# State-space layer with a mixture of experts: B and C rows spread over the partitions by one DMA each, and a different queue and place for three loads of the scan stage

## The reference, cut to what matters

```python
xi, res = split(x @ W_in);  xi = silu(causal_conv4(xi) + conv_b)
Bm, Cm = split(xi @ W_xproj)              # 16 + 16 numbers per token
delta = softplus(xi @ W_dt + b_dt);  A = -exp(A_log)
def step(h, inp):                         # one token after another
    u_i, d_i, B_i, C_i = inp
    dA = exp(d_i[:, None, :] * A[None, :, None])
    h = h * dA + d_i[:, None, :] * B_i[:, :, None] * u_i[:, None, :]
    return h, sum(h * C_i[:, :, None], axis=1)
y = (scan(step) + xi * D_param) * silu(res);  return y @ W_out
```

## Time and profile before

| | us |
|---|---|
| median of 2 runs | 8991.39 (8988.93 to 8993.84) |
| the profiled execution, its own time | 9033.67 |
| its span, on the slowest core (core 6) | 9032.1 |
| spans of the 8 cores | 8923.9 to 9032.1 |
| stage B on core 6, from the trace | 1938 to 6695 of the span |
| DVE busy, whole span | 4786.0 (53%) |
| PE busy, whole span | 3628.9 (40%) |
| the chain that ended last: DVE 46%, DMA 31%, PE 17% | |

### The profile page before, as it was taken

One profiled execution on the slowest core, in us unless ns is written; L12 is line 12 of the kernel. 1 busy time (PEld: TensorE's weight loads), 2 busy tenths in 40 slices (PEclk: granted clock), 3 DMA queues, 4 the chain that ended last, 5 costly groups with the idle time before them and its releaser, 6 DMA issues.

```text
span 9032.1 us, 43824 instructions; the slowest of 8 cores (8923.9 to 9032.1 us)
## 1 busy us (share of the span) xinstructions
PE 3628.9 (40%) x16374; PEld 1964.3 (22%) x16480; DVE 4786.0 (53%) x1407; ACT 1377.8 (15%) x1158; POOL 147.5 (2%) x213
## 2 busy tenths in 40 slices
PE   3886554520000000015345335435343348475665
PEld 2675444420000000002112112112110113132222
DVE  1211000018898888879889879779762222222222
ACT  0111111112222222222212112112110000000000
POOL 0000000000000000000000000000000000000000
PEclk9887777765555555557667667667676669797888
DMA  6334322231000111110120120120211148475664
GB/s 90 112 103 130 111 114 114 110 119 28 23 14 18 28 28 28 28 37 11 50 61 10 51 60 10 51 60 10 51 42 41 50 88 141 91 133 101 116 118 92
DMA packets 175006, 603.59 MB, mean 67 GB/s; under 512 B 38974, under 2 KB 56510, under 8 KB 146670
## 3 DMA queue, kind: packets, MB, share of 16 engines
q0 software_dynamic: 126752, 293.81, 16.8%
q1 hardware_dynamic: 48046, 306.98, 10.7%
HBM read 546.28 MB, written 168.43 MB: 79 GB/s over the span
## 4 chain that ended last, share of the span: by engine, by line
DVE 46%; DMA 31%; PE 17%; issue 3%; ACT 2%; another core or an unknown queue 1%; DVEq 0%; SPq 0%; POOLq 0%; ACTq 0%
DVE h_b L102 24%; DVE dBu L102 12%; DMA wr<-WrT 9%; DVE y_acc L102 6%; PE PP L490 5%; DMA Bb_b<-Bb_b 4%; DMA Cb_b<-Cb_b 3%; PE PP L896 2%; PE PP L382 2%; DMA u_b<-u_sp 2%; PE PP L437 1%; PE PP L397 1%; DMA wr<-WsT 1%; PE PP L717 1%; DMA du_sp<-du_b 1%
## 5 line engine op out<-in xcount | busy, mean ns | idle before, releaser
L626 PE MATMUL PP<-y_acc,sid 128*128 128x512 f32 x2048 | 1196.2, 750 | 3560.9 <-DVE y_acc L102 3560.9
L102 DVE TENSOR_TENSOR_SCAN h_b<-dAb,dBu 128x4112 f32<-128x4112 f32 x256 | 2233.4, 8724 | 197.5 <-ACT dBu L102 167.9
L626 PEld LDWEIGHTS PP<-y_acc,sid 128*128 128x128 f32 x2048 | 489.0, 246 | 4267.5 <-issue 4267.5
L102 DVE TENSOR_TENSOR dBu<-du_b,Bb_b 128x4096 f32<-128x4096 f32 x256 | 1132.8, 4425 | 419.7 <-DMA Bb_b<-Bb_b 392.9
L102 ACT ACTIVATE dAb<-d_b,A_bc 128x4096 f32<-128x4096 f32 x256 | 950.5, 3713 | 617.7 <-DMA d_b<-d_sp 594.5
L896 PE MATMUL PP<-ue,wr 128*128 128x512 bf16 x4012 | 913.0, 386 | 218.3 <-DVE ue L102 111.2
L490 PE MATMUL PP<-xib_b,wdt 128*128 128x256 bf16 x4096 | 516.7, 286 | 567.7 <-DMA u_b<-u_sp 484.3
L102 DVE TENSOR_TENSOR du_b<-d_b,u_b 128x4096 f32<-128x4096 f32 x16 | 70.8, 4425 | 1045.9 <-ACT d_b L102 1045.9
L102 DVE TENSOR_TENSOR y_acc<-h_b,Cb_b 128x4096 f32<-128x4096 f32 x128 | 566.4, 4425 | 14.1 <-DVE h_b L102 0.9
L896 PEld LDWEIGHTS PP<-ue,wr 128*128 128x128 bf16 x4096 | 403.0, 99 | 729.9 <-issue 274.2
L490 PEld LDWEIGHTS PP<-xib_b,wdt 128*128 128x128 bf16 x4096 | 418.6, 102 | 638.1 <-issue 571.8
(11 more groups left out here) (97 smaller groups left out, 1851.6 us busy)
## 6 DMA issues: line engine op xcount, KB each, us to landing
wr<-WrT POOLq DMA_DIRECT2D x64, 2048.0 KB, 15.2
u_sp<-u_b SPq DMA_DIRECT2D x20, 2048.0 KB
u_b<-u_sp SPq DMA_DIRECT2D x20, 2048.0 KB
d_sp<-d_b SPq DMA_DIRECT2D x16, 2048.0 KB
du_sp<-du_b SPq DMA_DIRECT2D x16, 2048.0 KB
d_b<-d_sp POOLq DMA_DIRECT2D x16, 2048.0 KB, 10.0
xib_sp<-xib_b SPq DMA_DIRECT2D x16, 1024.0 KB
sres_sp<-sres_b SPq DMA_DIRECT2D x8, 2048.0 KB
```

Source lines behind the costliest of these rows:

```text
L102: inst = fn(*a, **k)
L626: cT.inc(te.matmul(PP[:, zb * 512:(zb + 1) * 512], sid128[:], y_acc[:, zb * 512:(zb + 1) * 512], start=(n == 0), stop=(n == NST - 1)), 1 i ...
```

## The change

It edits two places of stage B. `bchain` becomes a single DMA, whose source repeats the same 16 rows of 256 tokens for each of the 128 partitions. And the loads into a real chunk are put in the same order as the others: SP issues only B; POOL issues `du_b`, `d_b`, and then, behind the wait for the last reader of C, the tile of C. `d_b` is no longer behind C, and `du_b` moves from SP's queue to POOL's.

```diff
         def bchain(q, ctr, buf, r0, win):
             ctr.inc(q.dma_start(
-                out=buf[0:1, :].rearrange("o (n t) -> o n t", n=NST),
-                in_=bc_hbm[r0:r0 + NST, win * TA:(win + 1) * TA][None]), 16)
-            for k in [1, 2, 4, 8, 16, 32, 64]:
-                q.wait_ge(ctr.sem, ctr.n)
-                ctr.inc(q.dma_start(out=buf[k:2 * k, :], in_=buf[0:k, :]), 16)
+                out=buf[:].rearrange("p (n t) -> p n t", n=NST),
+                in_=bc_hbm[r0:r0 + NST, win * TA:(win + 1) * TA][None]
+                .broadcast_to([128, NST, TA])), 16)
...
             if ch + 1 < NCH:
-                if ch + 1 < NRE:
-                    sy.wait_ge(cV.sem, dufree_V)
-                    bchain(sy, cS, Bb_b, 0, ch + 1)
-                    ld_S = cS.n
-                    ge.wait_ge(cV.sem, dufree_V)
-                    cL.inc(ge.dma_start(out=du_b[:], in_=du_sp[ch + 1]), 16)
-                    ld_L2 = cL.n
-                    ge.wait_ge(cA.sem, dfree_A)
-                    cL.inc(ge.dma_start(out=d_b[:], in_=d_sp[ch + 1]), 16)
-                    d_n, d_sem = cL.n, cL.sem
-                else:
-                    sy.wait_ge(cV.sem, dufree_V)
-                    cS.inc(sy.dma_start(out=du_b[:], in_=du_sp[ch + 1]), 16)
-                    bchain(sy, cS, Bb_b, 0, ch + 1)
-                    ld_S = cS.n
-                    ld_L2 = 0
+                sy.wait_ge(cV.sem, dufree_V)
+                bchain(sy, cS, Bb_b, 0, ch + 1)
+                ld_S = cS.n
+                ge.wait_ge(cV.sem, dufree_V)
+                cL.inc(ge.dma_start(out=du_b[:], in_=du_sp[ch + 1]), 16)
+                ld_L2 = cL.n
+                ge.wait_ge(cA.sem, dfree_A)
+                cL.inc(ge.dma_start(out=d_b[:], in_=d_sp[ch + 1]), 16)
+                d_n, d_sem = cL.n, cL.sem
+                if ch + 1 >= NRE:
                     ge.wait_ge(cV.sem, cV.n if real else dufree_V)
                     bchain(ge, cL, Cb_b, NST, ch + 1)
                     cb_L = cL.n
-                    ge.wait_ge(cA.sem, dfree_A)
-                    cL.inc(ge.dma_start(out=d_b[:], in_=d_sp[ch + 1]), 16)
-                    d_n, d_sem = cL.n, cL.sem
```

## The result

The changed kernel takes 9056.91 us (median of 27 runs), the kernel before 9014.63 (26 runs; at the time of the prediction there were two). The ratio is 1.0039, 95% interval 1.0020 to 1.0058: slower by 0.4%, where 8570 us and a range of 8520 to 8740 were forecast. The 421 us did not come in stage B itself; no other stage ate them. Outside stage B, core 6 has 4272 us in the profiled execution before and 4211 in the one after.

| stage B, us | core 0 | core 2 | core 4 | core 6 |
|---|---|---|---|---|
| before | 4748 | 4747 | 4748 | 4760 |
| after | 4628 | 4811 | 4833 | 4873 |

The account below looks back on a forecast made before the run. Stage B was taken as bound by DVE work (80.5% of its chain), with 742 us of loads as the ceiling; 133 + 32 + 35 + 221 = 421 us off 8991.4 gave 8570 us, range 8520 to 8740.

Parts of the forecast that it names:

- The 421 us: Whole gain forecast in stage B: 133 + 32 + 35 + 221 us, taking the median from 8991.4 to 8570.
- The new B load: how long?: Stage B's single broadcast load of B: 9 us alone, bounded by 6.2 us below and 29.5 (`bdt_c`) above.
- The sign that I had named for this case: Stage B: a lone `Cb_b` load well over 9 us, DVE waiting before `y_acc`, would speak for rivals two and three.
- Beside du_b and d_b: Three 2 MB tiles wanted at once at stage B's chunk boundaries share the DMA engines: 17 to 24 us together.
- Rival one: Stage B boundaries: POOL's loads starve B, which moves only after `d_b` has landed; gain 358 us, time 8632, chance 20%.
- the pair of rows 7 and 10: `xT` load: 7.72 us alone, 20.79 beside POOL's `wout` load; cited for rival one, neighbours slowing many small pieces.
- Chunks 0 to 7: Seven first-half boundaries of stage B: next scan at +27.5 us after the issue instead of +46.5, gain 133 us.
- the start, and into chunk 8: First scan of stage B and of chunk 8: 60.0 and 62.9 us after the issue become 27.5, gains 32 and 35.
- Chunks 8 to 15: Seven second-half boundaries of stage B: DVE's waits for B (63.0) and ACT (159.6), together 222.6 us, go; gain 221.
- The sum for a slow load, 802 - 16 T: Stage B's gain in us if each broadcast load takes T and is late everywhere; it loses from T = 50 on.
- rivals two and three: Stage B's one-source load is slow: T = 33, 8717 us, 14%; or at two engines' rate, T = 64, 9213 us, 9%.
- the 7% for no change: Chance given to a whole time within about 2% of before; a 5% chance lay between rivals two and three.

Follow-up runs that it names:

- the one-block kernel: Changed kernel, but each chunk's 16 rows in one 16 KB block of HBM, read as one piece per partition: 8622.97 us in a single run.
- with the chain: Changed kernel with the chain of eight copies put back, the new order of the queues kept: 8879.37 us, ratio 0.9821.
- the mended kernels: Changed kernel with rows relaid: 17 KB apart (8585.66 us, ratio 0.9534), 1.25 KB apart (8659.17), or one block per chunk (8622.97).
- with the copies: Changed kernel, but stage A writes 128 copies of all rows to HBM and each partition reads its own: 8950 us, writing included.

## Why the prediction was wrong

*The step that failed is the first one: "The new B load: how long?", 9 us, with 29.5 as the bound from above.* At the 90 GB/s that core 0 reached, its 2 MB take 23 us, at the 45 GB/s of core 6 they take 47; B's product started 54 us after the issue there, and lone C took 19 to 37. I drew the bound from pieces by their number and size and left out where they lie. `bdt_c` has 2048 small pieces, but no two partitions share one and all lie within 8 KB, so it bounded nothing here. And `gbig` was misread: its packet records show 128 pieces of 8192 bytes on the way in, not 2048 of 512, since each partition's 8 KB stand in a row in HBM. What would have been near is `xT`, with rows 16 KB apart too, and it is fast, 7.72 us: its 128 partitions read 128 different rows. Rows 16 KB apart were fast there, and a source shared by all partitions stood in no row at all. The sign that I had named for this case, a `Cb_b` load well over 9 us and a wait of DVE before `y_acc`, did come.

*"Beside du_b and d_b": right with the fast load, and the wrong way round with the slow one.* With a fast load the sum of 17 to 24 us for three tiles was good (+27.4 for the scan in the one-block kernel, against +27.5). Rival one had `du_b` starve B; what cost the time is that B starved `du_b`. I had noticed the pair of rows 7 and 10, and it holds for a part only: once both loads move, the large pieces do win, 229 GB/s against 15 in the shown stretch of core 6. But before that B is alone. The packet records show this with fast loads too: in every kernel with 2048 pieces of 1 KB, `du_b`'s first piece moves when 870 to 1280 of B's have started (medians by core), and in the one-block kernel after 80 of 128. So it is a share of B's load that goes first, and the delay follows B's rate: 4 to 6 us with the fast 1 KB loads, 5 to 8 at 16 KB + 256 bytes, 16 to 30 in the changed kernel, and 1 to 3 with the chain. `du_b`'s own time is 24 to 42 us beside the slow B, 10 to 15 beside a B of the mended kernels, 8.0 to 8.7 with none. My sum had no such delay; with a load of 9 us it is small, with one of 54 it also holds up `d_b` and ACT.

*Chunks 0 to 7, the start, and into chunk 8.* The arithmetic stands: the forecast leaves a wait of 33.2 - 19.0 = 14.2 us at a boundary, 114 for eight; with the pitch of 17 KB, DVE's waits for loads at the first eight are 108 us. *Chunks 8 to 15:* the 222.6 us did go to nothing in every kernel with a fast load, but for one wait of 6.2 us with the copies. *The sum:* 421 forecast; stage B is 418 and 430 us shorter on cores 0 and 6 with the pitch of 17 KB. The terms and their arithmetic hold once the load is fast; one input was off by a factor of two to six, and it is in all of them.

*The rivals.* The sum for a slow load, 802 - 16 T, gives no gain at T = 50, and the B load on core 6 sits at 54. That the formula meets the result there is in part luck: it has the same T for C, which took 19 to 37, and no starved `du_b`. On core 0, where B took 35 us, it gives a gain of some 240 us, and 120 came. So rivals two and three were the true mechanism's neighbours, and the 7% for no change, most of it from the stretch between them, holds the result. Both put the blame on many readers of one place, and that is half of it. The better hint was the sentence that I cited from the Trainium skill (DMA: Bandwidth & Descriptors, "Latency and other measured facts", on HBM rows a large power of two apart): I estimated 20 us from its figure, found that B would still be in time, and set it aside because `xT` ran at full rate at a pitch of 16 KB. The runs agree with the rule in kind and not in size: here 16 KB is enough when all partitions walk the same rows, the rate falls to 90 or 45 GB/s, and a pad of 256 bytes already brings 16.7 us.

*What stays open.* Why the rate is halved on some cores and in some chunks. The pattern goes by neighbours: in each of the pairs 0 and 1, 2 and 3, 4 and 5, 6 and 7, stage B of the two differs by 46 to 48 us (by 1 to 4 with the pitch of 17 KB). In the second half one core of the pair has the faster B (76 to 89 GB/s from 4 to 14 us after its issue) and the slower lone C (34 to 36 us), the other the slower B (mostly 40 to 64) and the faster C (19 to 23). Core 0's lone C took 36 us at first and 19.1 at last. Two neighbours that load at once from the same part of the memory would fit; but the traces of the cores have no common clock, and no run kept one core's loads apart from another's, so this is not shown. Nor is it shown how the memory maps addresses; the runs show only that 17 KB, 1.25 KB and one block are fast, 16 KB + 256 bytes half mended, 16 KB slow. And why `du_b` starts only when some 43 to 62% of B's pieces have started is not shown either, only that it does so with fast loads too.

## What to carry to other kernels

Before one DMA takes the place of a chain, ask of its source not only how many pieces and how large, but whether all partitions read the same rows, and how far apart these rows lie. If they share the rows and the pitch is 16 KB as here, pad the pitch by a row's piece (1 KB here) or lay the rows in one block; other pitches that are powers of two were not run. When a large edit moves nothing, undo it half by half: here one half gained 1.8% and the other lost 2.2%. And a load that is late for a fixed deadline can be cut in two and started when the first half of its tile is free; here its 19 to 35 us then cost nobody a wait.

## What the runs showed of the hardware

One source of 16 rows x 1 KB, read by 128 partitions, 2 MB in all, from issue to landing: 19 to 37 us at a row pitch of 16 KB, 16.7 at 16 KB + 256 bytes, 10.4 at 17 KB, 10.8 at 1.25 KB, and 7.4 as one piece of 16 KB; with a copy for each partition, 10.9 at 16 KB (medians of one core; the others lie within 1.5 us of them, but for the changed kernel). A slow load on SP's queue held up one issued half a microsecond later on POOL's for 16 to 30 us before its first piece (medians by core), although the DMA engines were 0.5 to 0.7 busy: `du_b` went from 8 us to as much as 42. In this program, whose cores took the same time for stage B within 15 us before, the slow load came with a spread of 245 us, and the slowest core is what is timed.
